# Graph attention by slots: order of the work within a slot, group of the weighting, length of the gather ring

## The chip, the cores and the metric

The kernel runs on one core of a Trainium2 chip. The metric is the device time in microseconds (us) of one execution. Engines are called by their names: TensorE (PE in the profile), VectorE (DVE), ScalarE (ACT), GpSimd (POOL) and SyncE (SP).

## What is computed

A stack of four graph layers over 3125 nodes of 256 features and 53125 edges: a weighted convolution with a small MLP, a second convolution that sums encoded edges, three blocks of typed attention (8 heads of 32) with an MLP each, and one last attention with edge features. Edges are sorted by their target. Cut to the step that matters, an attention over the edges that end in a node:

```python
score = (q[dst] * k[src]).sum(-1)                  # per edge and head
m     = segment_max(score, dst)
e     = exp(score - m[dst])
out   = segment_sum(e[:, :, None] * v[src], dst) / segment_sum(e, dst)
```

In the last layer the product is of a query with an edge's code, a term per source node is added, and a leaky ReLU stands before the maximum.

## The kernel before

Edges are packed into NT = 464 tiles of 128. Four tiles are a quad, four quads (WT = 16 tiles) a group; there are WG = 29 groups, so 116 quads. Each pair of tiles belongs to one block of 128 target nodes, whose number stands in a table (`c.block_i`) that engines read into registers at run time (`load_blocks`, L69). `attend` (L1399) is called four times: three typed calls, called L2a, and one with edge codes, called L3a. The instructions are written out in full; the code loops in Python only.

Per quad GpSimd gathers the rows of keys and values by four indirect DMAs (L1460) into a ring of `ring` buffers (10, or 11 in the last call), and waits for `weighted_ready` of the quad that held the buffer before. ScalarE widens two byte masks, `turned` (L1709) and `hot` (L1717). TensorE multiplies `turned` with the query block (`ask`, L1754), VectorE multiplies that with the gathered keys (`product`, L1513) and sums over a head (`reduce`, L1519). Per group a chain of maxima follows over 16 x 8 sequences of 128 edges: `flatten` (a transpose on TensorE, L1774), two scans (`scan_up` L1550, `scan_down` L1555), `spread_ends` (L1560), `sequence` on TensorE (L1779), two short scans along the group (`chain_up` L1566, `chain_down` L1572), `grow` (L1579), `expand` on TensorE (L1784), `pick_own` to `lower` (L1584 to L1604), and `unflatten` on TensorE (L1790, L1792). ScalarE takes the exponential (`soften`, L1729) and writes it into the extra columns of `weighted`. VectorE multiplies the gathered values with it (`weigh`, L1615), TensorE sums by target (`total`, L1765, two results per quad), VectorE adds each to the accumulator of its block (`add`, L1544) and, once per group, rescales one block (`rescale`, L1625).

Every engine has its order written out by hand. One pass of the loop is a slot. In slot n VectorE does the products and sums over heads of group n, the chain and the weightings of group m = n - 1, and additions of groups m - 1 and m. The chain's instructions stand one by one between additions and sums over heads; the four weightings follow in the second half of the slot, each followed by an addition, the rescale, or the next product. `weighted` holds one whole group, `prods` has two buffers and `score` one. TensorE's queries run two quads ahead of the product that reads them, and the totals of a quad follow its weighting.

## Time and profile before

| | |
|---|---|
| median of 3 runs | 5544.4 us (5542.47 to 5549.68) |
| profiled execution, span from first to last instruction | 6456.7 us |
| its own time beside the span | none given |
| instructions | 68859 |

The page gives, for the one profiled execution, the busy time of each engine and its share of the span, the busy share in 40 slices, the DMA queues, and groups of instructions with the mean duration of one, the idle time of the engine just before them and who ended most of it. The three runs of the table were taken apart from that execution.

### The profile page before, as it was taken

Reading aid. Unit: us, or ns where it says so; the run is one execution under the profiler, and the core shown is the slowest. Engines: PE = TensorE matmul, PEld = TensorE weight load, DVE = VectorE, ACT = ScalarE, POOL = GpSimd, SP = SyncE. Lnnn points to the kernel's source line nnn. Section 1 sums busy time; section 2 is a strip of 40 time slices with the busy share of each in tenths; the row PEclk is TensorE's granted clock in tenths of the full one; section 3 lists DMA queues with packets and bytes.
Section 4 is the critical chain, followed back from the end, with each engine's and each line's share of the span. In section 5 each row is a group of like instructions: output and inputs, shape, how many; then the busy total and the mean of one; then the engine's idle time right before and its main releaser. Section 6 shows DMA issues by size and latency. Waiting matters only on the chain. (4 is left out here: it accounts for less than half of the span.)

```text
span 6456.7 us, 68859 instructions
## 1 busy us (share of the span) xinstructions
PE 4457.4 (69%) x19341; PEld 3493.0 (54%) x19341; DVE 3832.0 (59%) x8692; ACT 1605.5 (25%) x3882; POOL 3364.1 (52%) x3108
## 2 busy tenths in 40 slices
PE   5666664577766666778857767796766679766776
PEld 4455453444436455557845555685555558545554
DVE  7544443544455666675347766643766776567777
ACT  3433332200004111113421211243211214312221
POOL 2588886366644555541356555134555530256663
PEclk9888887788888778779977777898778779878887
DMA  3688887255556555542266556315556541256664
GB/s 139 121 124 125 121 125 150 81 184 184 182 165 208 168 173 181 181 144 58 81 189 182 174 175 181 89 56 165 169 175 182 176 147 39 80 168 183 195 192 134
DMA packets 508435, 959.75 MB, mean 149 GB/s; under 512 B 85846, under 2 KB 298020, under 8 KB 507251
## 3 DMA queue, kind: packets, MB, share of 16 engines
q0 software_dynamic: 224512, 549.90, 34.1%
q1 hardware_dynamic: 283426, 404.92, 19.6%
q8 instruction: 170, 2.79, 0.2%
q14 instruction: 199, 1.62, 0.1%
q10 hardware_dynamic: 128, 0.52, 0.0%
HBM read 718.56 MB, written 236.50 MB: 148 GB/s over the span
## 5 line engine op out<-in xcount | busy, mean ns | idle before, releaser
L1460 POOL DMA_INDIRECT L2a_rows<-kv_rows,typed_index x960 | 966.3, 1007 | 627.8 <-DVE L2a_weighted L1615 349.9
L1765 PE MATMUL L2a_sums<-L2a_weighted,L2a_hot 128*128 128x264 f32 x2784 | 830.5, 450 | 166.8 <-DVE L2a_weighted L1615 159.4
L1754 PE MATMUL L2a_query<-x,L2a_turned 128*128 x2784 | 819.8, 447 | 55.8 <-ACT L2a_turned L1709 33.0
L867 POOL DMA_INDIRECT sum_rows<-L0s_rows,L0s_row_of x464 | 724.6, 1562 | 152.9 <-issue 119.4
L1765 PEld LDWEIGHTS L2a_sums<-L2a_weighted,L2a_hot 128*128 128x128 f32 x2784 | 591.2, 221 | 314.5 <-DVE L2a_weighted L1615 186.2
L1754 PEld LDWEIGHTS L2a_query<-x,L2a_turned 128*128 128x128 f32 x2784 | 627.2, 229 | 181.4 <-issue 62.5
L1460 POOL DMA_INDIRECT hold<-kv_rows,typed_index x432 | 445.4, 1031 | 449.8 <-DVE L2a_weighted L1615 279.5
L1460 POOL DMA_INDIRECT L3a_rows<-feature_rows,index x464 | 489.1, 1054 | 301.7 <-DVE L3a_weighted L1615 155.1
L1285 POOL DMA_INDIRECT L1s_rows<-rows,index x464 | 451.0, 972 | 351.2 <-issue 133.8
L1717 ACT ACTIVATE L2a_hot<-L2a_hot 128x512 f32<-128x512 uint8 x348 | 218.7, 629 | 1470.8 <-PE L2a_sums L1765 726.6
L1002 PE MATMUL L0s_message<-features,L0s_share 128*128 x928 | 312.8, 496 | 285.9 <-ACT L0s_share L967 285.9
L2296 POOL TENSOR_SCALAR L2d_here<-hold,mask 128x256 f32<-128x256 f32 x200 | 183.1, 933 | 552.6 <-DVE hold L2372 404.5
L1342 PE MATMUL L1s_code_ps<-L1s_wide,L1s_fields 128*128 128x512 f32 x464 | 285.8, 702 | 219.3 <-DVE L1s_code L1311 138.4
L1519 DVE TENSOR_REDUCE L2a_score<-L2a_prods 128x32 f32<-128x1024 f32 x348 | 417.8, 1201 | 0.4
L1002 PEld LDWEIGHTS L0s_message<-features,L0s_share 128*128 128x128 f32 x928 | 215.3, 242 | 364.9 <-issue 329.1
L1765 PE MATMUL L3a_sums<-L3a_weighted,L3a_hot 128*128 128x264 f32 x928 | 282.7, 457 | 92.6 <-DVE L3a_weighted L1615 89.3
L1709 ACT ACTIVATE L2a_turned<-L2a_turn 128x512 f32<-128x512 uint8 x348 | 216.9, 624 | 507.7 <-PE L2a_query L1754 191.8
L1513 DVE TENSOR_TENSOR L2a_prods<-L2a_query,L2a_rows 128x1024 f32<-128x1024 f32 x240 | 291.9, 1216 | 76.5 <-remote 47.3
L901 DVE TENSOR_TENSOR L0s_hot<-count,early 128x512 f32<-128x512 f32 x116 | 80.5, 694 | 419.0 <-ACT L0s_hot L980 412.7
L1305 DVE TENSOR_TENSOR acc<-acc,L1s_sums 128x256 f32 x232 | 97.4, 420 | 378.4 <-remote 176.5
L1544 DVE TENSOR_TENSOR acc<-acc,L2a_sums 128x264 f32 x696 | 290.4, 417 | 10.8 <-PE L2a_sums L1765 9.1
L1615 DVE TENSOR_TENSOR L2a_weighted<-L2a_rows,L2a_weighted 128x1024 f32<-128x1024 f32 x240 | 292.4, 1218 | 3.4 <-ACT L2a_weighted L1729 1.3
(428 smaller groups left out, 8550.9 us busy)
## 6 DMA issues: line engine op xcount, KB each, us to landing
code_rows<-L1s_code SPq DMA_DIRECT2D x116, 512.0 KB
L3a_code<-code_rows SPq DMA_DIRECT2D x116, 512.0 KB
L0s_wide<-source_rows SPq DMA_DIRECT2D x116, 256.0 KB
L2a_turn<-turned_rows SPq DMA_DIRECT2D x87, 256.0 KB
L2a_pens<-mask_rows SPq DMA_DIRECT2D x87, 256.0 KB
L2a_hot<-hot_rows SPq DMA_DIRECT2D x87, 256.0 KB
kv_rows<-L2d_key_rows SPq DMA_DIRECT2D x50, 384.0 KB, 2.6
kv_rows<-L2d_value_rows SPq DMA_DIRECT2D x150, 128.0 KB, 2.4
```

The costliest lines, as they stand in the source:

```text
L867: pool.indirect_dma_start(c.sum_rows[u], bass.IndirectOffsetOnAxis(ap=row_of[:, 4 * n + u:4 * n + u + 1], axis=0), rows[n % ring][:, u, :] ...
L1002: last = pe.matmul(message[n % 2][:, u, :], share[n % 2][:, u, :], at(c.q, b[i])[:, 0:D], start=True, stop=True)
L1285: pool.indirect_dma_start(rows[n % ring][:, u, :], None, table, bass.IndirectOffsetOnAxis(ap=c.index[:, t:t + 1], axis=0)).then_inc(landed ...
L1342: pe.matmul(code_ps[j % 2][:, :, :].rearrange("p k d -> p (k d)"), fields[g % 2][:, :], wide[:, 2 * j % FT:2 * j % FT + 2, :].rearrange("p ...
L1460: pool.indirect_dma_start(rows[n % ring][:, u, :], None, table, bass.IndirectOffsetOnAxis(ap=index_of[:, t:t + 1], axis=0)).then_inc(lande ...
L1513: dve.tensor_tensor(prods[q % 2][:, :, :], query[q % 2][:, :, :], other, ALU.mult).then_inc(multiplied, 1)
L1519: last = dve.tensor_reduce(own.rearrange("p k h -> p (k h)"), prods[q % 2][:, :, :].rearrange("p k (h d) -> p (k h) d", h=H), AX.X, ALU.add)
L1544: dve.tensor_tensor(at(c.acc, b), at(c.acc, b), sums[(m * WP + j) % held][:, :], ALU.add).then_inc(added, 1)
L1615: dve.tensor_tensor(weighted[:, 4 * q:4 * q + 4, :].rearrange("p k (h d) -> p k h d", h=H)[:, :, :, 0:HD], rows[quad % ring][:, :, values: ...
L1717: act.activation(hot[quad % 2][:, :, :].rearrange("p u e -> p (u e)"), hot8[m % 2][:, q * 4 * P:(q + 1) * 4 * P], ACT.Copy).then_inc(hot_r ...
L1754: last = pe.matmul(query[q % 2][:, u, :], turned[quad % 2][:, u, :], at(c.q, b[2 * q + u // 2]), start=True, stop=True)
L1765: last = pe.matmul(sums[(m * WP + j) % held][:, :], hot[quad % 2][:, j % 2 * 2 + k, :], weighted[:, 2 * j + k, :], start=k == 0, stop=k == 1)
```

## The change

The loops over groups become loops over quads, and each slot of VectorE becomes four stretches that all begin in the same way. A product is followed directly by its sum over heads, from a single `prods` buffer; two additions stand together; the chain of the previous group is cut into three: both long scans and the ends behind the first quad, the short scans and the gap behind the second, the rest behind the third. The weighting works two groups (8 quads, `late`) behind the product, where it was one group behind, and comes before the product of its stretch (after it in the fourth). `weighted` becomes three buffers of one quad (`kept`), and the exponentials get tiles of their own (`prob`, two), from which ScalarE copies the extra columns (`column`). The shrink factors are copied from PSUM by ScalarE (`keep_shrink`) before VectorE's `rescale` reads them. `score` gets two buffers. The ring becomes 12 buffers (13 in the last call). TensorE's queries stay two quads ahead, between the two totals of a quad. SyncE's loads of edge codes are spread over the slot. The loop runs WG + 3 times on VectorE. In `load_blocks` VectorE reads 8 values per slot, where it read 16. `reduce` of the last call holds the small addition that was `join`. The core of the diff:

```diff
-    held, codes = 3, 4
+    held, codes, late, kept, quads = 3, 4, 2 * WQ, 3, WG * WQ
     with Stage(nc, name) as st:
-        ring = RQ if typed else 11
+        ring = 12 if typed else 13
...
-        weighted = st.sb("weighted", [P, WT, VC])
-        prods = [st.sb(f"prods{k}", [P, 4, D]) for k in range(2)]
-        score = st.sb("score", [P, WT, H])
+        weighted = [st.sb(f"weighted{k}", [P, 4, VC]) for k in range(kept)]
+        prods = st.sb("prods", [P, 4, D])
+        score = [st.sb(f"score{k}", [P, WT, H]) for k in range(2)]
+        prob = [st.sb(f"prob{k}", [P, WT, H]) for k in range(2)]
...
+            def product(g):
+                if g < quads:
+                    wait(dve, query_ready, g + 1)
+                    wait(dve, score_ready if typed else summed, g)
+                    if typed:
+                        wait(dve, landed[g % ring], 64 * (g // ring + 1))
+                        other = rows[g % ring][:, :, 0:D]
+                    else:
+                        wait(dve, code_landed[g % codes], 16 * (g // codes + 1))
+                        other = code[g % codes][:, :, :]
+                    dve.tensor_tensor(prods[:, :, :], query[g % 2][:, :, :], other, ALU.mult).then_inc(multiplied, 1)
+            def reduce(g):
+                if g < quads:
+                    n, q = g // WQ, g % WQ
+                    wait(dve, multiplied, g + 1)
+                    own = score[n % 2][:, 4 * q:4 * q + 4, :]
+                    last = dve.tensor_reduce(own.rearrange("p k h -> p (k h)"),
+                                             prods[:, :, :].rearrange("p k (h d) -> p (k h) d", h=H), AX.X, ALU.add)
+                    if typed:
                         last.then_inc(score_ready, 1)
...
+            def add(w, k, b):
+                if 0 <= w < quads:
+                    j = 2 * w + k
+                    wait(dve, sums_ready, j + 1)
+                    wait(dve, added, j)
+                    if w % WQ == 0 and k == 0:
+                        wait(dve, rescaled, w // WQ)
+                    dve.tensor_tensor(at(c.acc, b), at(c.acc, b), sums[j % held][:, :], ALU.add).then_inc(added, 1)
...
+            def weigh(w):
+                if 0 <= w < quads:
+                    q = w % WQ
+                    wait(dve, prob_ready, w // WQ + 1)
+                    wait(dve, sums_ready, 2 * (w - kept + 1))
+                    dve.tensor_tensor(
+                        weighted[w % kept][:, :, :].rearrange("p k (h d) -> p k h d", h=H)[:, :, :, 0:HD],
+                        rows[w % ring][:, :, values:values + D].rearrange("p k (h d) -> p k h d", h=H),
+                        prob[w // WQ % 2][:, 4 * q:4 * q + 4, :].unsqueeze(3).broadcast_to([P, 4, H, HD]), ALU.mult
+                    ).then_inc(weighted_ready, 1)
...
+            for n in range(WG + 3):
+                m, g = n - 1, n * WQ
+                chain, tail = 0 <= m < WG, n >= 2
+
+                if tail:
+                    blocks = load_blocks(nc, mybir.EngineType.DVE, c, (n - 2) * WP - 2, WP)
+                else:
+                    blocks = [0] * WP
+                weigh(g - late)
+                product(g)
+                reduce(g)
+                add(g - late - 1, 0, blocks[0])
+                add(g - late - 1, 1, blocks[1])
                 if chain:
                     scan_up(m)
                     scan_down(m)
                     spread_ends(m)
+                weigh(g + 1 - late)
+                product(g + 1)
+                reduce(g + 1)
+                rescale(n - 2, blocks[2])
+                add(g - late, 0, blocks[2])
+                add(g - late, 1, blocks[3])
                 if chain:
                     chain_up(m)
                     chain_down(m)
                     grow(m)
+                weigh(g + 2 - late)
+                product(g + 2)
+                reduce(g + 2)
+                add(g + 1 - late, 0, blocks[4])
+                add(g + 1 - late, 1, blocks[5])
                 if chain:
                     pick_own(m)
                     join_own(m)
                     reach_first(m)
                     reach_last(m)
                     spread_fall(m)
                     lower(m)
+                product(g + 3)
+                reduce(g + 3)
+                weigh(g + 3 - late)
+                add(g + 2 - late, 0, blocks[6])
+                add(g + 2 - late, 1, blocks[7])
...
+            def keep_shrink(m):
+                if 0 < m < WG:
+                    wait(act, shrink_ready, m)
+                    wait(act, rescaled, m - 1)
+                    act.activation(shrink[:, :], shrink_ps, ACT.Copy).then_inc(shrink_kept, 1)
+
+            def column(w):
+                if 0 <= w < quads:
+                    q = w % WQ
+                    wait(act, prob_ready, w // WQ + 1)
+                    wait(act, sums_ready, 2 * (w - kept + 1))
+                    act.activation(weighted[w % kept][:, :, HD::HC], prob[w // WQ % 2][:, 4 * q:4 * q + 4, :], ACT.Copy
+                                   ).then_inc(column_ready, 1)
...
+                total(g - late, 0)
+                ask(g + 2, near[0], near[1])
+                total(g - late, 1)
+                sequence(m)
+                total(g + 1 - late, 0)
+                ask(g + 3, near[2], near[3])
+                total(g + 1 - late, 1)
+                expand(m)
+                total(g + 2 - late, 0)
+                ask(g + 4, near[4], near[5])
+                total(g + 2 - late, 1)
+                unflatten(m)
+                ask(g + 5, near[6], near[7])
+                flatten(n)
+                total(g + 3 - late, 0)
+                total(g + 3 - late, 1)
```

## Rows read from the trace of the kernel before

**Rows 1.** The page of the kernel before: span, and busy time by engine.
```profile
span 6456.7 us, 68859 instructions
PE 4457.4 (69%) x19341; PEld 3493.0 (54%) x19341; DVE 3832.0 (59%) x8692; ACT 1605.5 (25%) x3882; POOL 3364.1 (52%) x3108
```

**Rows 2.** Busy time by stretch, middle of first and last attention call.
```profile
core 0: us, PE busy (x) PEld busy (x) DVE busy (x) ACT busy (x) POOL busy (x), PEclk, DMA share, GB/s
2200.00:2880.00 680.00, 479.17 (x1748) 370.89 (x1747) 471.72 (x802) 132.28 (x243) 392.25 (x385) 0.79 0.59 177
...
5750.00:6400.00 650.00, 455.96 (x1767) 356.97 (x1766) 489.21 (x928) 135.56 (x244) 407.53 (x383) 0.82 0.63 188
```

**Rows 3.** Timeline: a small TensorE matmul and the VectorE scan waiting for it.
```profile
2512.62 0.22 PE L1779 MATMUL L2a_small<-L2a_ends,head 128*8 128x32 f32 x2
...
2520.60 0.27 DVE L1566 TENSOR_TENSOR_SCAN L2a_up<-links,L2a_up,L2a_small 8x32 f32<-8x32 f32 x1 [6.79 <-remote]
```

**Rows 4.** Timeline of GpSimd, sixteen gathers of one slot and the next first.
```profile
2499.98 0.94 POOL L1460 DMA_INDIRECT hold<-kv_rows,typed_index  x1 [7.21 <-DVE L2a_weighted L1615]
2501.23 1.90 POOL L1460 DMA_INDIRECT hold<-kv_rows,typed_index  x1 [0.30 <-issue]
...
2519.91 0.94 POOL L1460 DMA_INDIRECT L2a_rows<-kv_rows,typed_index  x1 [0.30 <-issue]
2528.45 0.94 POOL L1460 DMA_INDIRECT L2a_rows<-kv_rows,typed_index  x1 [7.59 <-DVE L2a_weighted L1615]
```

**Rows 5.** Waits of GpSimd: first call, last call, then everything before attention.
```profile
POOL L2a_rows L1460 <- DVE L2a_weighted L1615: 116.6, 16, 7.8
...
POOL hold L1460 <- DVE L2a_weighted L1615: 92.0, 11, 18.5
...
POOL L3a_rows L1460 <- DVE L3a_weighted L1615: 155.1, 27, 22.0
...
POOL L1s_rows L1285 <- remote: 62.1, 25, 6.7
POOL L1s_rows L1285 <- PE L1s_sums L1353: 27.6, 22, 2.7
POOL sum_rows L867 <- ACT L0s_rows L961: 21.9, 34, 11.9
POOL sum_rows L867 <- DMA sum_rows<-L0s_rows,L0s_row_of: 11.6, 38, 0.3
```

**Rows 6.** Timeline of VectorE: neighbours that don't depend on each other.
```profile
2533.64 1.22 DVE L1519 TENSOR_REDUCE L2a_score<-L2a_prods 128x32 f32<-128x1024 f32 x1
2534.77 1.22 DVE L1615 TENSOR_TENSOR L2a_weighted<-L2a_rows,L2a_weighted 128x1024 f32<-128x1024 f32 x1
2535.90 0.42 DVE L1544 TENSOR_TENSOR acc<-acc,L2a_sums 128x264 f32 x1
2536.24 1.22 DVE L1513 TENSOR_TENSOR L2a_prods<-L2a_query,L2a_rows 128x1024 f32<-128x1024 f32 x1
```

**Rows 7.** Timeline of VectorE: dependent neighbours, at fill, first chain, and the end.
```profile
2073.59 1.23 DVE L1513 TENSOR_TENSOR L2a_prods<-L2a_query,hold 128x1024 f32<-128x1024 f32 x1 [2.67 <-DMA hold<-kv_rows,typed_index]
2074.84 1.22 DVE L1519 TENSOR_REDUCE L2a_score<-L2a_prods 128x32 f32<-128x1024 f32 x1
...
2121.16 0.42 DVE L1550 TENSOR_TENSOR_SCAN L2a_climb<-L2a_pens,L2a_small 128x128 f32<-128x128 f32 x1 [14.21 <-remote]
2121.61 0.42 DVE L1555 TENSOR_TENSOR_SCAN L2a_most<-L2a_pens,L2a_climb 128x128 f32<-128x128 f32 x1
...
2124.29 0.20 DVE L1566 TENSOR_TENSOR_SCAN L2a_up<-links,L2a_small 8x32 f32<-8x32 f32 x1
2124.53 0.21 DVE L1572 TENSOR_TENSOR_SCAN L2a_tops<-links,L2a_up 8x32 f32<-8x32 f32 x1
...
2907.65 0.43 DVE L1544 TENSOR_TENSOR acc<-acc,L2a_sums 128x264 f32 x1 [0.21 <-DVE acc L1544]
2908.29 0.43 DVE L1544 TENSOR_TENSOR acc<-acc,L2a_sums 128x264 f32 x1 [0.21 <-DVE acc L1544]
```

More of the change, by code:

```diff
@@ L1425, in attend @@
         gap, fall, diag = st.sb("gap", [H, 1]), st.sb("fall", [H, 1]), st.sb("diag", [H, H])
+        shrink = st.sb("shrink", [P, H])
         pick, other = st.sb("pick", [P, 2, WT]), st.sb("other", [P, 2])
@@ new lines, in load_code @@
+            def load_code(g):
+                if not typed and g < quads:
+                    wait(sp, multiplied, g - codes + 1)
+                    sp.dma_start(code[g % codes][:, :, :], c.code_rows[:, 4 * g:4 * g + 4, :]
+                                 ).then_inc(code_landed[g % codes], 16)
+            load_turn(0)
+            for g in range(codes - 1):
+                load_code(g)
+            load_turn(1)
+            for n in range(WG + 1):
+                load_code(n * WQ + 3)
+                load_pens(n)
+                load_code(n * WQ + 4)
+                load_hot(n - 1)
+                load_code(n * WQ + 5)
+                load_turn(n + 2)
+                load_code(n * WQ + 6)
@@ L1674, in _ @@
                     lower(m)
-                if more:
-                    product(n, 2)
-                if tail:
-                    add(m - 1, 7, before[7])
-                if chain:
-                    weigh(m, 0)
-                    rescale(m, now[0])
-                if more:
-                    reduce(n, 2)
-                if chain:
-                    weigh(m, 1)
-                    add(m, 0, now[0])
-                if more:
-                    product(n, 3)
-                    join(n, 2)
@@ new lines, in column @@
+            def column(w):
+                if 0 <= w < quads:
+                    q = w % WQ
[3 more added lines that the diff above has]
+                                   ).then_inc(column_ready, 1)
+            for g in range(3):
+                turn(g)
+            for n in range(WG + 2):
+                m, g = n - 1, n * WQ
+                for s in range(WQ):
+                    widen(g + s - late + 1)
+                    turn(g + s + 3)
+                    if s == 2:
+                        drop(m)
+                    if s == 3:
+                        soften(m)
+                        keep_shrink(m)
+                    column(g + s - late + 1)
@@ new lines, in total @@
+            def total(w, k):
+                if 0 <= w < quads:
+                    j = 2 * w + k
+                    wait(pe, weighted_ready, w + 1)
+                    wait(pe, column_ready, w + 1)
+                    wait(pe, hot_ready, w + 1)
+                    wait(pe, added, j - held + 1)
+                    for u in range(2):
+                        last = pe.matmul(sums[j % held][:, :], hot[w % 2][:, 2 * k + u, :],
+                                         weighted[w % kept][:, 2 * k + u, :], start=u == 0, stop=u == 1)
@@ L1827, in _ @@
-            for j in range(6, WP):
-                total(WG - 1, j)
+                if 0 <= m < WG:
+                    wait(pe, zz_ready, m + 1)
+                    if m:
+                        wait(pe, diag_ready, m)
+                        pe.matmul(shrink_ps, first_hot[m % 2][:, :], diag[:, :], start=True, stop=True
+                                  ).then_inc(shrink_ready, 1)
+                    pe.transpose(below_ps, zz[:, :], c.ident[:, :]).then_inc(below_ready, 1)
+            near = load_blocks(nc, mybir.EngineType.PE, c, 0, WQ)
```

297 lines of the change are left out of this document (79 added, 218 removed).

## The prediction

> **What bounds the kernel now.** I read the page's totals first, then the busy times by stretch, the waits of GpSimd, the timeline of one slot on GpSimd, VectorE and TensorE, and last the starts of neighbouring VectorE instructions, which give prices.
>
> The page shows a span of 6456.7 us with VectorE at 59% and GpSimd at 52% [rows 1]. The median of the three runs shown is 5544.4 us. The page gives no other time for the profiled execution than its span, so 912.3 us lie between the profiled execution and a plain one, and before anything is priced one has to know where they sit. In 680 us in the middle of the first attention call GpSimd issued 385 gathers, which is 24.1 slots of 16, so a slot took 28.2 us; VectorE was busy 471.7 us of it, 19.6 us per slot [rows 2]. In the last call (feature rows) 383 gathers in 650 us give 27.2 us per slot, VectorE 20.4 us.
>
> What is VectorE doing in the other 8 us? In the slot at 2512 us the little matmul of line 1779 stands at 2512.62 us for 0.22 us, and the scan that waits for nothing but it starts at 2520.60 us, after 6.79 us idle with no releaser that this trace can name ("remote") [rows 3]. The same kind of gap sits before the scan or before the pick of line 1584 in almost every slot. TensorE's update comes late, although its record does not.
>
> GpSimd shows what this costs. One slot of gathers runs from 2499.98 us, mostly 0.95 us each with 0.30 us between two of them (one of them 1.90 us), to 2520.85 us, and then GpSimd waits 7.59 us for a weighting to free a buffer [rows 4]. So a slot of gathers takes 20.0 us (16 x 1.25) to 21.2 us (20.87 plus 0.30); I take 20.8. Those waits sum to 116.6 + 92.0 = 208.6 us in the first call and 155.1 us in the last; the second and third calls are built like the first, so 3 x 208.6 + 155.1 = 781 us. The gathers and scatters of the two layers before them add 62.1 + 27.6 + 21.9 + 11.6 = 123 us of waiting on the same engine [rows 5]. The sum, 904 us, is almost exactly the missing 912 us. I read this as follows: the late TensorE updates belong mainly to the profiled execution, and in a plain one the attention calls run at GpSimd's rate, 20.8 us per slot (21.3 us in the last call, where a gather means 407.5 / 383 = 1.06 us against 392.3 / 385 = 1.02 us [rows 2]), with VectorE's 19.6 us plus its own short waits just below it. That is the base from which I price the change.
>
> The Trainium skill (NOTIFIC — the notification-queue block, section 7.1 Overflow) says that the internal pipeline that writes trace records never drops one and may hold up the engine instead. That fits the gap, with its 6.79 us beside it, but no row shows the cause, and no term below uses it.
>
> **The change, part by part.** Everything that the change removes from VectorE is waiting; the arithmetic stays: four products, four sums over heads, four weightings, eight additions, one rescale and one chain of maxima per slot. What changes is who stands next to whom, and that has a price in this trace.
>
> Independent neighbours overlap. A sum over heads starts at 2533.64 us, a weighting at 2534.77, an addition at 2535.90, a product at 2536.24: 1.13, 1.13 and 0.34 us from start to start, each about 0.08 us before its forerunner's record ends [rows 6]. Dependent neighbours do not. A product followed at once by its own sum takes 1.25 us to the next start, so 0.12 us more. Two additions in a row whose sums are there take 0.64 us (2907.65 to 2908.29), so 0.30 us more: the second waits for the first's count and only then works out its block's address. The two scans in a row take 0.45 us (2121.16 to 2121.61), about 0.12 us more than their overlapping neighbours by the same pattern, and the two short scans 0.24 us (2124.29 to 2124.53), about 0.1 us more [rows 7].
>
> - **Products next to their sums, one product buffer.** 4 x 0.12 = 0.48 us per slot. The wait for the previous sum costs nothing, because a weighting of 1.13 us lies between (three quads of four) or 2 us of chain.
> - **Additions in pairs.** Four pairs, 4 x 0.30 = 1.20 us. The rescale now stands directly ahead of the first addition of its group, which waits for it: another 0.30 us (bounds 0.1 and 0.3).
> - **The chain in thirds.** Scan on scan and ends on scan, 2 x 0.12 = 0.24 us; the short scans and the gap about 0.15 us.
> - **Register loads of the block table.** 8 values instead of 16 on VectorE. The load used to be mostly hidden; now it stands behind an addition that itself waits, so I expect it in the open, 0 to 0.7 us, taken as 0.2 us, as no row of the groups shows it alone.
> - **ScalarE** gets four column copies and one copy of the shrink factors per slot. It is busy 132 us in 680, 5.5 us per slot [rows 2]; even 5 x 0.4 us leaves it under 8 us. Behind its new waits stand the widenings and turnings, each two quads early. I cost it at nothing; what hides it is VectorE's 22 us.
> - **TensorE** does the same matmuls and queries now run two quads ahead of the product that reads them. By the order written out, every result is asked for at least 4 us after its matmul is issued. Cost nothing; if that cover went, its busy 479 us in 680, 19.9 us per slot at the granted mean of 0.79 [rows 2], would be next.
> - **Longer ring and SyncE's order.** GpSimd gets 12 or 13 buffers, of which 8 quads are held by the later weighting: four to five quads, 20 us, of lead. Its own work stays at 20.8 us. The loads keep a group's lead. Nothing.
>
> Sum for VectorE in a typed call: 19.6 + 0.48 + 1.50 + 0.39 + 0.2 = 22.2 us; adding the same starts instruction by instruction through the new slot gives 21.9. I take 22.0 us. In the last call the small addition after each sum becomes its direct neighbour too, 4 x 0.12, so from 20.4 us it goes to 23.1 us (the sum is 20.4 + 2.6 + 0.5 = 23.5, I shade it by the same 0.3).
>
> Against the gatherer's 20.8 and 21.3 us the slot becomes longer by 1.2 and 1.8 us. The first two slots of a call run at GpSimd's rate in either kernel, so 27 slots count: 3 x 27 x 1.2 + 27 x 1.8 = 97 + 49 = 146 us. The end of a call gets longer as well: after the last product the old kernel has one chain, four weightings and their additions, some 19 us; the new one has eight weightings and sixteen additions, about 12.5 + 10 + 2 = 24.5 us. That is 5.5 x 4 = 22 us. Together 168 us. Taking the trace's own time as the base of the gatherer's rate instead (28.2 less the 7.6 us wait, 20.6 us per slot) moves this by 20 us either way. 5544.4 + 168 is 5712; I write 5710 us.
>
> **Weighing a rule.** The Trainium skill (VectorE: DVE Perf Modes, section The DRAIN you can't avoid) says that a next VectorE instruction starts only when the pipe is empty and that a semaphore between two adds nothing. Rows 6 and 7 disagree: 1.13 us without the dependence, 1.25 us with it. By the rule all the neighbour terms would be nil and the result would be that of the first rival.
>
> **The rivals.**
> *GpSimd keeps the bound.* If dependent neighbours cost nothing in the new order, VectorE needs 19.6 us, stays under 20.8 us, and only the longer end counts: 5544 + 22 = 5566 us, or 5545 if the end hides as well. Against it: the 0.64 us between additions repeats. Chance 0.13. The skill's DRAIN rule, named above, would lead here.
> *The late updates are real.* If TensorE's updates come late in plain runs too, say by half of the 7.6 us, a slot now takes 24.5 us; the new order asks for each result 4 to 10 us later than it is issued and would swallow that, so a slot falls to 22.2 us: 27 x 4 x 2.3 = 248 us gained, less 22, about 5320 us. It decides from the point where the present plain slot exceeds 22 us. For it: rows 3 show a wait that really held VectorE. Against it: GpSimd's waits already fill the 912 us, and no other place in the trace could give back that much. At a quarter instead of a half the two kernels tie. Chance 0.22, and about 0.05 more for a tie.
> *TensorE becomes the bound.* At the lower of its clock's two levels (1.2 and 2.4 GHz) its matmuls would need over 30 us per slot; if the new gaps lower the granted mean from 0.79 to 0.7, it needs 22.5 us plus waits: 5800 us and more. Chance 0.08.
> That the change doesn't do what it says (weighting not late) can be excluded by the diff.
>
> **How the numbers follow.** The forecast has 0.52 and a range of its own from 5630 us (no load shown, rescale at 0.1 us, slots of 21.4 us) to 5800 us (load at 0.7 us, gathers at 20.0 us so that VectorE's about 20.4 us was the old bound). The range for 8 in 10 takes in the first rival and about half of the faster one: 5430 to 5810 us. A measurement of this kernel can tell about 0.2% from no change, 11 us. Slower by more: forecast, TensorE case and most of the first rival, 0.72; within: 0.06; faster: 0.22.
>
> **What would show it.** In the profile after: VectorE's additions 0.64 us apart in pairs and product to sum 1.25 us; VectorE busy share up, its waits before the scan and the pick gone or much smaller; slots of the profiled execution shorter than 28.2 and 27.2 us, because the slack swallows the late updates, although the plain time rises; GpSimd still waiting for weightings. It is wrong if plain time falls: then the plain runs had waits that I ascribe to the profiled execution alone.

## The result and the profile after

| | before | after |
|---|---|---|
| median, same chip | 5547.0 us (4 runs, 5542.5 to 5551.9) | 5863.7 us (4 runs, 5860.6 to 5864.9) |
| ratio | 1 | 1.0567, 95% interval 1.0552 to 1.0582 |
| span of the profiled execution | 6456.7 us | 5861.4 us |

The change makes the kernel 5.7% slower, by 317 us, where 166 us (5710 less 5544.4) were forecast. The profiled execution of the kernel after is no special one: its own time is 5863.05 us. That of before was (6456.7 us against 5544.4 us), and run e1 below takes its place. The page's totals of the kernel after, where [rows 1] stood for before:

```profile
span 5861.4 us, 71363 instructions
PE 4302.7 (73%) x19341; PEld 3231.5 (55%) x19341; DVE 3960.7 (68%) x8692; ACT 1645.1 (28%) x4458; POOL 3428.9 (58%) x3108
```

Busy time by stretch, in the middle of the first and of the last attention call (the columns are those of [rows 2]):

```profile
2200.00:2600.00 400.00, 309.38 (x1239) 217.33 (x1237) 349.01 (x565) 98.44 (x255) 295.08 (x275) 0.98 0.75 215
5300.00:5600.00 300.00, 225.28 (x853) 155.33 (x854) 258.68 (x448) 68.72 (x180) 199.58 (x190) 0.95 0.66 200
```

From the start of the third product of one slot to that of the next, the mean over the 27 steady slots of a call is 23.3 us in the three typed calls and 25.2 us in the last. VectorE is busy 87% of the first stretch; TensorE's granted clock is 0.98 there, near the upper level (2.4 GHz). Who waits for whom in the first call (us in total, times, longest):

```profile
DVE L2a_weighted L1625 <- PE L2a_sums L1761: 34.2, 22, 1.6
DVE acc L1552 <- DVE acc L1552: 19.8, 92, 0.6
...
POOL L2a_rows L1462 <- DVE L2a_weighted L1625: 26.9, 18, 1.6
```

GpSimd waits for VectorE, and VectorE waits for two things only: 0.21 us between the additions of a pair, as priced, and 1.6 us once per slot before a weighting. The profile puts the latter down to TensorE's results. The timeline of VectorE at that place shows what it is:

```profile
2502.19 1.22 DVE L1530 TENSOR_REDUCE L2a_score<-L2a_prods 128x32 f32<-128x1024 f32 x1
2503.33 1.21 DVE L1625 TENSOR_TENSOR L2a_weighted<-L2a_rows,L2a_prob 128x1024 f32<-128x1024 f32 x1
2504.46 0.42 DVE L1552 TENSOR_TENSOR acc<-acc,L2a_sums 128x264 f32 x1
2505.09 0.43 DVE L1552 TENSOR_TENSOR acc<-acc,L2a_sums 128x264 f32 x1 [0.21 <-DVE acc L1552]
2507.08 1.23 DVE L1625 TENSOR_TENSOR L2a_weighted<-hold,L2a_prob 128x1024 f32<-128x1024 f32 x1 [1.55 <-PE L2a_sums L1761]
```

The additions stand 0.63 us apart. From the second one to the weighting it is 1.99 us, and between them the program has nothing but `load_blocks`. The trace keeps a record of the register load itself, which the profile doesn't count as busy: 1.84 us for 8 values. TensorE's results were there before: the second addition had already waited for a later one than the weighting needs. The view of line 71, `load_blocks`, has these loads, as minimum, median and maximum in ns. In the kernel before, where they are of 16 values, and in the kernel after:

```profile
L71 DVEq TENSOR_LOAD <-block_i x29: 597/1100/1118, 2088.8 to 2891.7; - x29
...
L71 DVEq TENSOR_LOAD <-block_i x28: 1840/1846/1853, 2061.6 to 2669.9; - x28
```

In the last call the sum over heads, its small addition (L1538) and the leaky ReLU (L1543) wait for one another:

```profile
5402.49 1.22 DVE L1530 TENSOR_REDUCE L3a_score<-L3a_prods 128x32 f32<-128x1024 f32 x1
5403.81 0.19 DVE L1538 TENSOR_TENSOR L3a_score<-L3a_score,L3a_rows 128x32 f32<-128x32 f32 x1
5404.04 0.29 DVE L1543 SCALAR_TENSOR_TENSOR L3a_score<-L3a_score 128x128 f32<-128x128 f32 x1
```

That is 1.32 us from the sum to its addition and 0.23 us from there on, 0.3 us per quad more than 1.13 us [rows 6] and some 0.1 us (an estimate) for independent neighbours.

### The profile page after: what moved, and what is told of

Same layout as the page of the kernel before. It is cut to its first block and busy times, and to the rows that moved or that the text cites. A ratio compares the mean times of both kernels' runs of the same rounds, so it can differ in the third digit from the quotient of the medians.

```text
span 5861.4 us, 71363 instructions
## 1 busy us (share of the span) xinstructions
PE 4302.7 (73%) x19341; PEld 3231.5 (55%) x19341; DVE 3960.7 (68%) x8692; ACT 1645.1 (28%) x4458; POOL 3428.9 (58%) x3108
## 5 line engine op out<-in xcount | busy, mean ns | idle before, releaser
L1462 POOL DMA_INDIRECT L2a_rows<-kv_rows,typed_index x1032 | 1103.1, 1069 | 385.1 <-issue 297.1
L1761 PE MATMUL L2a_sums<-L2a_weighted,L2a_hot 128*128 128x264 f32 x2784 | 773.0, 407 | 292.0 <-DVE L2a_weighted L1625 273.5
L1749 PE MATMUL L2a_query<-x,L2a_turned 128*128 x2784 | 753.8, 418 | 162.1 <-DVE L2a_prods L1523 97.5
L1761 PEld LDWEIGHTS L2a_sums<-L2a_weighted,L2a_hot 128*128 128x128 f32 x2784 | 505.0, 194 | 475.3 <-DVE L2a_weighted L1625 366.1
L1749 PEld LDWEIGHTS L2a_query<-x,L2a_turned 128*128 128x128 f32 x2784 | 540.9, 204 | 349.3 <-issue 278.3
L1462 POOL DMA_INDIRECT hold<-kv_rows,typed_index x360 | 375.8, 1044 | 152.7 <-issue 152.7
L1625 DVE TENSOR_TENSOR L2a_weighted<-L2a_rows,L2a_prob 128x1024 f32<-128x1024 f32 x258 | 313.8, 1216 | 89.7 <-PE L2a_sums L1761 89.4
L1353 PE MATMUL L1s_sums<-L1s_rows,L1s_hot 128*128 128x256 f32 x928 | 255.0, 399 | 136.9 <-issue 107.9
L1761 PE MATMUL L3a_sums<-L3a_weighted,L3a_hot 128*128 128x264 f32 x928 | 267.8, 419 | 115.4 <-DVE L3a_weighted L1625 101.8
L1353 PEld LDWEIGHTS L1s_sums<-L1s_rows,L1s_hot 128*128 128x128 f32 x928 | 174.2, 196 | 297.5 <-issue 224.1
L1749 PE MATMUL L3a_query<-hold,L3a_turned 128*128 x928 | 257.7, 426 | 46.3 <-DVE L3a_prods L1523 24.8
```

Source lines behind the costliest of these rows:

```text
L1353: last = pe.matmul(sums[j % held][:, 0:D], hot[n % hots_held][:, u, :], rows[n % ring][:, u, :], start=k == 0, stop=k == 1)
L1462: pool.indirect_dma_start(rows[g % ring][:, u, :], None, table, bass.IndirectOffsetOnAxis(ap=index_of[:, t:t + 1], axis=0)).then_inc(lande ...
L1625: dve.tensor_tensor(weighted[w % kept][:, :, :].rearrange("p k (h d) -> p k h d", h=H)[:, :, :, 0:HD], rows[w % ring][:, :, values:values ...
L1749: last = pe.matmul(query[g % 2][:, u, :], turned[g % 2][:, u, :], at(c.q, second if u // 2 else first), start=True, stop=True)
L1761: last = pe.matmul(sums[j % held][:, :], hot[w % 2][:, 2 * k + u, :], weighted[w % kept][:, 2 * k + u, :], start=u == 0, stop=u == 1)
```

## The experiments

Each time is compared with the kernel before on the same chip and in the same batch of runs. Runs e1 to e8 share one chip, e9 to e11 a second, e12 to e15 a third, e16 and e17 a fourth.

**e1: the kernel before, profiled again.** No edit.

> The kernel before, unchanged, for a second profile. The record's theory (the late TensorE updates belong to that one profiled execution, a plain one runs at GpSimd's rate): a span near 5545 us, slots of 20.8 us in the typed calls and 21.3 us in the last, and hardly any wait of GpSimd for a weighting. First rival (the late updates come with every profiled execution of this order): a span near 6450 us again. Second rival (VectorE, not GpSimd, holds the plain slot): a span near 5545 us with GpSimd still waiting 1 us or more in each slot.

It took 5558.9 us (5548.3 us the median of seven others) with a span of 5557.2 us: profiling costs at most 0.2%. Totals by stretch, then the waits of VectorE and of GpSimd in the first call:

```profile
2200.00:2600.00 400.00, 332.86 (x1367) 256.41 (x1366) 367.94 (x636) 106.72 (x189) 296.62 (x296) 0.93 0.77 231
5300.00:5600.00 300.00, 191.42 (x763) 146.51 (x761) 228.84 (x424) 57.31 (x103) 163.44 (x157) 0.90 0.56 170
...
DVE L2a_prods L1513 <- DMA L2a_rows<-kv_rows,typed_index: 22.5, 21, 2.8
DVE L2a_prods L1513 <- DMA hold<-kv_rows,typed_index: 7.6, 7, 2.1
...
POOL L2a_rows L1460 <- issue: 85.0, 279, 0.3
POOL hold L1460 <- issue: 36.6, 120, 0.3
```

GpSimd never waits for anybody, VectorE waits for the gathered rows, and no update of TensorE comes more than 0.9 us after its instruction. For the profile of [rows 3] the updates can't tell this: that trace has 45827 records of semaphore changes and this one 84800, and some of VectorE's and ScalarE's are missing too. The starts can. There the scan behind `sequence` begins in the median 2.9 us, and up to 8.0 us, after both its matmul and VectorE's instruction before it have ended, and the pick behind `expand` 4.2 us, and up to 8.6 us; in e1 neither is ever over 0.1 us late. The slot is 20.9 us in the typed calls and 21.5 us in the last. So GpSimd sets the pace, at the rates that the prediction took as its base, but the 912 us don't come from profiling.

**e2: the register load aligned.** The places of the table are counted from its start, where four spare ones (`GP`) stand ahead of the first block. The kernel after loads eight values that begin 2 past a multiple of 8; e2 loads ten from the multiple of 8 itself, of which the last eight are used.

```diff
-                    blocks = load_blocks(nc, mybir.EngineType.DVE, c, (n - 2) * WP - 2, WP)
+                    blocks = load_blocks(nc, mybir.EngineType.DVE, c, (n - 2) * WP - GP, WP + 2)[2:]
```

> The changed kernel, where VectorE's register load starts two values earlier, on a multiple of eight, and takes ten values instead of eight. Theory (the load of 1.84 us is long because of where it starts, and 1.55 us of it are idle time of VectorE in each of 116 slots): the load takes 0.6 to 1.1 us as the other loads do, the idle time falls to 0.4 to 0.8 us, the kernel to 5735 to 5775 us. Rival (the length goes with VectorE's state, or the wait is for TensorE's totals as the profile names it): the load stays at 1.8 us or the idle time stays, 5850 to 5870 us.

5784.4 us, ratio 1.0420 (1.0402 to 1.0437). That is 9 us above the range expected. The load takes 1.07 us instead of 1.84 us for two more values, and the slot falls by 0.7 to 0.8 us, to 22.6 us (24.4 us in the last call): here each microsecond of the load is a microsecond of the slot. In the attention calls of these traces VectorE's loads take 0.6 us for 8 values and 1.10 us for 16, both from 4 past a multiple of 8, 1.07 us for 10 from a multiple of 8, and 1.84 us for 8 from 2 past one. So every short one starts on a multiple of 4. Start and length aren't all of it: in the layer before attention the loads of 8 values from 4 past a multiple of 8 take anything from 0.59 to 1.65 us, and no run shows why.

**e3: the load hidden.** The same load, issued after the fourth sum of the slot before, where VectorE has work queued that doesn't need it.

```diff
-                if tail:
-                    blocks = load_blocks(nc, mybir.EngineType.DVE, c, (n - 2) * WP - 2, WP)
-                else:
-                    blocks = [0] * WP
+                blocks = following
...
+                if 1 <= n < WG + 2:
+                    following = load_blocks(nc, mybir.EngineType.DVE, c, (n - 1) * WP - GP, WP + 2)[2:]
                 weigh(g + 3 - late)
```

> The changed kernel with the same aligned load issued before the fourth weighting of the slot before, where a weighting of 1.13 us and a sum cover it. Theory (exposed load is the term that was mis-sized, 1.63 us per slot): all of it goes, 116 x 1.63 = 189 us, to about 5675 us; VectorE's slot 21.7 us and 23.6 us in the last call. Rival (something else stands behind it at once, such as TensorE's totals): 5735 us or more.

5812.3 us, ratio 1.0470 (1.0452 to 1.0487), 0.5% slower than e2, where 5675 us were expected: a miss. VectorE's own work is less, but the slot is 22.9 us. GpSimd is the one that holds it (16 x (1.13 + 0.30) = 22.9 us), because its gathers grew. Its timeline next to VectorE's weightings, then its totals of 500 us (busy, mean ns | idle before), which in e1 are 1003 ns:

```profile
2511.46 1.22 DVE L1625 TENSOR_TENSOR L2a_weighted<-hold,L2a_prob 128x1024 f32<-128x1024 f32 x1
2511.68 1.82 POOL L1462 DMA_INDIRECT L2a_rows<-kv_rows,typed_index  x1 [0.30 <-issue]
2513.80 0.94 POOL L1462 DMA_INDIRECT L2a_rows<-kv_rows,typed_index  x1 [0.30 <-issue]
...
L1462 POOL DMA_INDIRECT L2a_rows<-kv_rows,typed_index x264 | 298.0, 1129 | 80.5 <-issue 80.5
L1462 POOL DMA_INDIRECT hold<-kv_rows,typed_index x86 | 97.5, 1134 | 26.2 <-issue 26.2
```

A gather that starts 0.2 us after a weighting takes 1.82 us, that is until 0.8 us after the weighting has ended; the next takes 0.94 us. Over the 500 us gathers that overlap a weighting mean 1.42 us, the others 0.97 us. Wherever within a weighting a gather starts, it ends 0.82 us after the weighting (102 gathers of e3's first call, nine in ten of them within 0.01 us of it). Which of them meet depends on how the two engines' rhythms fall on each other, and so the order of VectorE sets the price of a gather.

**e4: dependent neighbours apart**, the load in its old place and length. One addition moves between each product and its sum, the rescale ahead of its product.

```diff
+                add(g - late - 1, 0, blocks[0])
                 reduce(g)
-                add(g - late - 1, 0, blocks[0])
                 add(g - late - 1, 1, blocks[1])
...
```

> The changed kernel with the first addition of each pair between the product and its sum over heads, and the rescale ahead of the product; late weighting, ring, chain in thirds and the misaligned load stay. Theory (a dependent neighbour costs 0.12 us at a product and 0.29 us at an addition): 4 x 0.12 + 4 x 0.29 + 0.2 = 1.8 us per slot, and as the last addition no longer holds the instruction queue, about 1 us of the load is covered too, so the slot would be 20.4 us and meets GpSimd's 20.8 us: 5560 to 5600 us. Rival (the rule that a semaphore between two VectorE instructions adds nothing): at most 20 us gained, 5845 us.

5618.7 us, ratio 1.0127 (1.0110 to 1.0144). Over three quarters of the loss are gone, with not one instruction fewer. That is not the neighbours alone: VectorE goes from the last addition of a slot to the weighting of the next in 0.34 us, where the kernel after took 1.99 us, although the load between them still takes 1.84 us.

```profile
2271.89 0.41 DVE L1552 TENSOR_TENSOR acc<-acc,L2a_sums 128x264 f32 x1
2272.23 1.21 DVE L1625 TENSOR_TENSOR L2a_weighted<-hold,L2a_prob 128x1024 f32<-128x1024 f32 x1
```

The record of this load runs from 2269.94 to 2271.78 us, while VectorE is at the sum and the weighting ahead of these two. So this order hides the whole load, where about 1 us of it was expected. The time is 19 us above the upper expectation, because the slot (21.3 us) is GpSimd's now, with gathers of 1.02 us.

**e5: the kernel before with half of the sums' work left out.** The sums over heads read 16 of 32 products.

```diff
-                                         prods[q % 2][:, :, :].rearrange("p k (h d) -> p (k h) d", h=H), AX.X, ALU.add)
+                                         prods[q % 2][:, :, :].rearrange("p k (h d) -> p (k h) d", h=H)[:, :, 0:HD // 2],
+                                         AX.X, ALU.add)
```

> The kernel before, where the sum over a head (line 1519) adds 16 of its 32 products: part of the computation left out, so that VectorE has about 0.55 us less to do four times per slot, 2.2 us of its 19.3 us. Theory (GpSimd's gathers hold the slot at 21 us, VectorE only waits longer for rows): no more than 0.5% off, 5520 to 5560 us. Rival (VectorE's own chain holds it): 116 x 1.4 to 2.2 us less, 5290 to 5385 us.

5693.9 us, ratio 1.0248 (1.0216 to 1.0280): less work for VectorE makes the kernel slower, which neither side had expected. Its waits and GpSimd's totals:

```profile
DVE L2a_prods L1513 <- DMA L2a_rows<-kv_rows,typed_index: 71.0, 44, 4.8
...
L1460 POOL DMA_INDIRECT L2a_rows<-kv_rows,typed_index x250 | 274.2, 1097 | 76.2 <-issue 76.2
```

VectorE waits for rows three times as long as in e1 (94.8 against 30.1 us, both row buffers together), and the gathers mean 1.09 us instead of 1.00 us: those that meet a weighting meet it earlier in its course and are held up longer.

**e6 and e7: the weights of the weighting out of SBUF.** e7 lets ScalarE write them to PSUM, so that the weighting has one SBUF input; that leaves room for two result buffers only, and e6 is the kernel before with two (`held`), its control.

```diff
-    held, codes = 3, 4
+    held, codes = 2, 4
...
-                    weighted[:, 4 * q:4 * q + 4, HD::HC].unsqueeze(3).broadcast_to([P, 4, H, HD]), ALU.mult
+                    prob_ps[:, 4 * q:4 * q + 4, :].unsqueeze(3).broadcast_to([P, 4, H, HD]), ALU.mult
```

> The kernel before with two PSUM buffers for the totals instead of three: the control for the next run, which needs the third bank. Both theories: the same or up to 3% slower, 5545 to 5710 us; the gathers' lengths unchanged (mean 1.00 us).

> The control, and ScalarE writes the exponentials a second time, into the freed PSUM bank, from which VectorE's weighting reads them: one SBUF input instead of two, the same arithmetic. Theory (a gather that meets a weighting is held up by it, since both want the same way into SBUF, 1.4 us against 0.97 us without in the run with the hidden load): the gathers all take 0.95 us, GpSimd's slot falls from 21.0 to 20.1 us, and the kernel is 40 to 100 us faster than the control. Rival (long gathers come from full DMA queues): lengths as in the control, and the kernel 10 to 40 us slower than it, for the second exponential of 0.4 us in the chain.

e6 took 5669.2, 5669.7 and 5705.7 us (ratio 1.0233, 1.0190 to 1.0275); a fourth one took 12633 us, is left out and stays unexplained. e7 took 5661.0 us (1.0182, 1.0159 to 1.0204). In e7 the gathers take 947 ns in the mean, against 1010 ns in e6, and 2 of 372 take over 1 us. So a weighting with both inputs in SBUF is what stretches them. The time hardly moves: the intervals of the two ratios overlap, and 40 to 100 us were expected. With two result buffers VectorE waits for the maxima in both ("DVE L2a_pick <- PE L2a_small" 51.9 us in 24 times in e6, 43.5 us in 25 times in e7, absent in e1), and in e7 GpSimd waits for weightings: this order with two buffers can't use the faster gathers.

The Trainium skill (SBUF — State Buffer, section SBUF: two separate sides) describes such a lock: VectorE and GpSimd share a pair of ports, and of an instruction of VectorE with two SBUF inputs and one of GpSimd that reads SBUF, whichever starts first has the pair for its whole length, while the other waits. The rows agree for the gather, which reads its row numbers from a table in SBUF: one that starts within a weighting waits for its end. By the page the gather shown above would lose the time to the end of the weighting, 1.0 us (an estimate); it loses 0.87 us (1.82 less 0.95). For the other half the rows don't agree: 47 weightings of e3's first call start while a gather runs, and they start no later and take no longer (1.21 us) than the others.

**e8: e4 and e3 together.**

> The changed kernel with neighbours apart and the load aligned and hidden, both edits together. VectorE needs about 19.7 us a slot by the two earlier runs. Theory (from there on GpSimd holds the slot, and its gathers are stretched by weightings): no better than with the neighbours apart alone, 5570 to 5640 us, VectorE waiting 1 to 2 us per slot for rows. Rival (VectorE still holds it): 116 x 0.4 us less than with the neighbours apart alone, 5570 us, and with a GpSimd that keeps 20.8 us per slot, 5545 us.

5656.0 us, ratio 1.0169 (1.0149 to 1.0190), slots of 21.4 us, gathers of 1.03 us: 16 us above the range expected and 0.4% above e4. The load was hidden in e4 already, and the floor is GpSimd's, so there was nothing left for this edit to gain.

**e9 to e11: the mended order**, on a chip where the kernel before takes 6488.2 us (6470 to 6497). e9 is e8 with the join of the last call apart from its sum and the fourth weighting ahead of the fourth product; e10 adds the weights in PSUM to it, with two result buffers; e11 is e5 with the weights in PSUM and two result buffers.

> The changed kernel with four edits to VectorE's order: neighbours apart, load aligned and hidden, the fourth weighting ahead of its product, and the small addition of the last call behind an addition of totals instead of directly behind its sum over heads (there 1.30 us from start to start). Weightings still read two SBUF tiles. Theory (GpSimd with stretched gathers holds the typed calls; only the last call gets better, by up to 1.2 us in 29 slots): 5600 to 5650 us. Rival (VectorE's order is all that matters): below the kernel before, 5500 to 5540 us.

> The same, and the weighting reads the exponentials from a PSUM bank of their own, which the totals give up (two buffers instead of three); ScalarE copies them there once per group. The same arithmetic. Theory (a weighting with two SBUF inputs stretches gathers; with one it doesn't, and the later weighting gives TensorE's results room enough for two buffers): gathers of 0.95 us, 20.0 us of GpSimd per slot, VectorE 19.6 to 20.8 us: a slot of 20.2 us, 21 us in the last call, 5440 to 5490 us, faster than the kernel before. Rival (two buffers for the totals make VectorE wait as they did in the old order): 5560 us or more, with waits for totals of 1 us and more per slot.

> The kernel before with sums over 16 of 32 products (part of the computation left out), two buffers for the totals, and the exponentials read from PSUM. With the short sums alone the kernel took 5694 us and its gathers 1.09 us in the mean. Theory (that slowdown is gathers held up by weightings, which came closer together): gathers of 0.95 us, GpSimd's slot 20.0 us, kernel 5440 to 5500 us. Rival (the short sums cost time in some other way, such as colder TensorE or full DMA queues): 5640 us or more.

6252.8 us (ratio 0.9634, 0.9618 to 0.9650), 6361.3 us (0.9802, 0.9786 to 0.9819) and 7202.3 us (1.1096, 1.1077 to 1.1114). Readers of TensorE's results start late in these traces too; waits of VectorE in e9:

```profile
DVE acc L1557 <- remote: 70.0, 23, 5.0
DVE acc L1557 <- PE L2a_sums L1770: 39.0, 29, 4.5
```

158 of its 928 additions of totals start over 1 us, and up to 6.7 us, after both their matmul and VectorE's instruction before have ended; in e1, e8 and the kernel after no update of TensorE comes over 0.9 us late. The 6488 us are unprofiled runs, so such times come in any execution on such a chip. That the 6457 us of the profile of before come from one too is likely, not shown: the record doesn't name its chip. An order with more lead between a matmul and its reader is better there (e9), with one result buffer fewer less so (e10), and the old order with short sums, weights in PSUM and two result buffers is far worse (e11).

**e12 to e15: the same again**, on a chip where the kernel before takes 5544.9 us; e12 is the kernel after.

> The changed kernel, unaltered. If the chip has no late TensorE updates (kernel before at 5545 to 5560): 5864, ratio 1.057 as in the result. If it has them (kernel before at 6450 to 6500): theory A, that the kernel before pays for them because its sums wait for a product and its weighting for a result of TensorE only just done, while the changed order has two groups of slack, expects a ratio below 1, 6200 to 6400 us, ratio 0.96 to 0.99. Theory B, that late updates cost both orders alike, expects about 6800, ratio 1.05.

> The changed kernel with its register load aligned and issued a step earlier, its dependent neighbours of VectorE apart, and its join of the last call apart from its sum (the edit of e9). Chip without late updates: theory A, VectorE's own work sets the slot, expects VectorE at 19.6 busy and 20.3 per slot, 5480 to 5540. Theory B, the gathers stretched by the weightings set a floor of 21.3 to 21.5 per slot as in e4 and e8, expects 5600 to 5650, ratio 1.010 to 1.018. Chip with late updates: as e9, ratio 0.963.

> The same, with the weights of the weighting read from PSUM, where ScalarE copies them (the edit of e10). Chip without late updates: theory B expects that gathers of 0.95 us give the floor back, 20.2 to 20.8 per slot, 5440 to 5560, ratio 0.98 to 1.0; theory A, which gives the weightings no part in it, expects no difference from e13 within 0.3%. Chip with late updates: as e10, ratio 0.980.

> The kernel before with the sums of 16 of its 32 products per slot left out, and the weights of the weighting read from PSUM (the edit of e11). Chip without late updates: if stretched gathers were all that made e5 slower than before, the slot is GpSimd's own 20.2 us and the time 5400 to 5500, ratio 0.975 to 0.99. If a chain through TensorE and ScalarE that the product's buffers close is the floor besides, as e7's waits of the pick for the maxima suggest, 5600 to 5680, ratio 1.01 to 1.025, with VectorE waiting for the maxima or for rows and GpSimd waiting for weightings. Chip with late updates: as e11, ratio 1.11.

| | us | ratio, 95% interval | slot typed, last | gathers |
|---|---|---|---|---|
| e12 after | 5871.0 | 1.0586 (1.0569 to 1.0604) | 23.3, 25.2 | 1.07 us |
| e13 mended order | 5635.9 | 1.0153 (1.0119 to 1.0186) | 21.6, 22.4 | 1.06 us |
| e14 with weights in PSUM | 5472.8 | 0.9865 (0.9849 to 0.9882) | 20.1, 20.5 | 0.95 us |
| e15 before, half sums, PSUM | 5511.4 | 0.9939 (0.9922 to 0.9956) | 20.6, 20.9 | 0.95 us |

e13 shows the floor of the stretched gathers, as its theory B had it, and e14 lifts it: 163 us between them for the place of one operand, in spite of one result buffer fewer and one more copy on ScalarE. GpSimd's rows of e14, totals and then waits:

```profile
L1465 POOL DMA_INDIRECT L2a_rows<-kv_rows,typed_index x304 | 288.3, 948 | 92.6 <-issue 90.8 <-DVE L2a_weighted L1633 1.8
...
POOL L2a_rows L1465 <- DVE L2a_weighted L1633: 1.8, 6, 0.3
```

16 x (0.95 + 0.30) = 20.0 us is its slot, and VectorE is busy 385.2 of 400 us in it: both are full. This version is faster than both kernels. e15 undoes the loss of e5 (from 1.0248 to 0.9939), though it too has one result buffer fewer. Against e7, from which it differs in the short sums alone, they gain 2.4% (1.0182 to 0.9939); with stretched gathers the same edit lost 2.5% (e5). It is 11 us slower than expected, and its VectorE waits for the maxima (56.0 us in 26 times), as in e6 and e7.

**e16 and e17: the weights in PSUM for the kernel after, and for e3.** Two result buffers again.

> The changed kernel with nothing altered but the place from which the weighting reads its weights: a copy in PSUM, made by ScalarE. Theory A, the changed kernel is held by VectorE's own instructions and its exposed register load, 23.3 us per slot, and the stretched gathers lie in GpSimd's spare time: gathers of 0.95 us, GpSimd waits longer for weightings (about 3 us per slot), time unchanged within 0.5%, 5840 to 5890, ratio 1.053 to 1.062. Theory B, that the gathers' stretching is part of the slowdown, expects 5650 to 5750, ratio 1.02 to 1.037.

> The changed kernel with its register load issued a step earlier (the edit of e3) and the weights read from PSUM. Theory A, in e3 the slot was held by gathers that the weightings stretched: gathers of 0.95 us, VectorE at 20.4 us busy with its short gaps gives 21.0 to 21.5 us per slot, 22.5 to 23 in the last call, 5640 to 5700, ratio 1.017 to 1.028. Theory B, e3 was held by something else (a cycle of buffers through TensorE and ScalarE), expects e3's 22.9 us per slot again and 5790 to 5830, ratio 1.044 to 1.051.

e16: 5909.4 us, ratio 1.0642 (1.0615 to 1.0668). The gathers are at 0.95 us and the kernel after gains nothing; it is 19 us above the upper expectation and loses another 0.5 us per slot, since with two result buffers the additions wait for TensorE ("DVE acc <- PE L2a_sums" 17.3 us in 22 times, absent in the kernel after). So the stretched gathers are no part of the slowdown as it stands. e17: 5741.8 us, ratio 1.0354 (1.0327 to 1.0380), neither theory's number. The slot is 21.9 us, against 22.9 us in e3, and GpSimd waits for VectorE again, 2 us per slot. The place of the load, on VectorE's timeline:

```profile
2504.62 0.43 DVE L1555 TENSOR_TENSOR acc<-acc,L2a_sums 128x264 f32 x1 [0.21 <-DVE acc L1555]
2504.97 1.21 DVE L1628 TENSOR_TENSOR L2a_weighted<-L2a_rows,L2a_own_bank 128x1024 f32<-128x1024 f32 x1
```

0.35 us instead of 1.99 us. So the gathers did hold e3, as theory A had it. The expected time was too low because VectorE's slot without its load is 21.9 us, not 21.0 to 21.5 us, and in the last call, where the joins hold VectorE, 24.5 us, not 22.5 to 23 us.

## Why the prediction was right in direction and wrong in size

- **Base of 20.8 and 21.3 us per slot, GpSimd's rate**: right, 20.9 and 21.5 us in e1.
- **"The late TensorE updates belong mainly to the profiled execution"**: wrong. GpSimd's waits did fill the 912 us, so they sat where the prediction put them, but that doesn't say why. e1 has none although it is profiled, and unprofiled runs on another chip are as slow. What was taken for one kernel in two modes was most likely one kernel on two chips (the chip of the first profile isn't on record). The number for the base survived, since the median came from an undisturbed chip. The note on trace records that was set beside it explains nothing here.
- **Neighbours: 0.48 us for products, 1.20 for additions, 0.30 for the rescale, 0.39 for the chain**: right. Product to sum is 1.25 us, addition to addition 0.63 us, scan to scan 0.45 us; rescale to addition is 0.56 us, 0.22 more than the 0.34 of independent ones. With the load taken out and the gathers freed (e17) the typed slot is 21.9 us, and the 22.0 us of the prediction less its 0.2 us for the load are 21.8. In the typed calls e14 differs from e17 only in VectorE's order, with the neighbours of products, sums and additions apart and the fourth weighting ahead of its product, and its slot is 20.1 us, GpSimd's floor: at least 1.8 us are theirs. The 245 us that come back in e4 are neighbours and load together.
- **Register load, 0.2 us, bounds 0 to 0.7**: this is the term that was mis-sized. That it would stand in the open was foreseen; its length was wrong. It costs 1.55 us per slot, twice its upper bound. What was missed is the start: 16 values of the kernel before took 1.10 us, but these 8 start 2 past a multiple of 8 in the table and take 1.84 us. 22.0 - 0.2 + 1.55 = 23.35 us; measured 23.3. The groups of the page have no row of the load, but the view of line 71 has one. For the layer before attention of the kernel before, where the loads are of 8 values, it shows 28 of them from 0.59 to 1.65 us, and that would have been a wider bound. In the attention calls of the kernel before the load is hidden (VectorE's idle time behind it is 0 in the median), so no idle time there could show its price.
- **Last call, 0.12 us per quad for the join**: 0.3 us, two waits in a row instead of one. 23.1 + 1.35 + 0.72 = 25.2 us; measured 25.2.
- **End of a call, 5.5 us more**: from the last product to the last addition it is 23.9 us before and 31.8 us after, 7.9 us more (7.6 in the last call), partly the same load.
- **GpSimd's "own work stays at 20.8 us"**: wrong as a rule, harmless here. Its gathers mean 1.08 us instead of 1.00 in the kernel after, 22.1 us per slot, still under VectorE's 23.3.
- **TensorE, ScalarE, ring, SyncE at nothing**: right; neither VectorE nor GpSimd waits for them (the wait laid to TensorE is the load), and TensorE's granted clock rose from 0.93 to 0.98 in the first call.
- **The sum**: 97 + 49 + 22 = 168 us predicted. Measured (23.29 - 20.94) x 81 = 190, (25.21 - 21.53) x 27 = 99, ends 32: 321 us by these parts, 316 us by the four calls from first product to last addition, 317 us in the medians.
- **Rivals.** GpSimd doesn't keep the bound, and by the Trainium skill's DRAIN rule (VectorE: DVE Perf Modes, The DRAIN you can't avoid) a semaphore between two adds nothing and the neighbour terms would be nil, which the starts above and e14 against e17 contradict. The same section says that a next instruction that isn't held starts earlier, and with that the 1.13 us of independent neighbours agree. The late updates are real in plain runs, but on another chip; there the mended order gains 3.7%, as that rival argued. Whether the change itself gains there wasn't tried. TensorE didn't become the bound.

So the step that failed is the register load's 0.2 us, with bounds of 0 and 0.7 us that came from no row: the 1.35 us that it lacked, times 108 slots, are 146 us, and the range left 100 us above the forecast.

## What to carry to other kernels

A wait or a gap that is moved into the open has to be priced by its own length, also where the profile doesn't count it: register loads first of all, with their start and length. The order of the neighbours decides whether it is in the open: the same load of 1.84 us costs 1.55 us behind an addition that waits for its neighbour, and nothing in e4. When the bound is shared by two engines, an instruction of one can lengthen those of the other, so less work on one may cost time (e5): look at the mean duration of the same instruction in both traces. And a profiled span far from the median calls for a second profile before any of it is used as the base.

## What the runs showed of the hardware

- In the attention calls a register load on VectorE takes 0.6 us for 8 values and 1.10 us for 16 from 4 past a multiple of 8 in the table, 1.07 us for 10 from a multiple of 8, and 1.84 us for 8 from 2 past one. In the layer before, loads of 8 took 0.59 to 1.65 us from the same kind of start, cause open. The waits give the gap to the wrong releaser.
- An indirect gather issued on GpSimd takes 0.95 us alone. If it starts within a weighting with both inputs in SBUF it ends 0.82 us after the weighting, so that it takes up to 2.0 us. A weighting that starts within a gather is not held up. With one input in PSUM the gathers mean 0.95 us.
- On one chip of four VectorE started up to 6.7 us (e9) after a matmul that it needed and its own instruction before had ended (6488 us instead of 5545 to 5557 us for the kernel before, the chip's cause unknown), and kernels rank differently there: e10 is behind e9 by 1.7%, where on another chip e14, the same kernel as e10, is ahead of e13, the same as e9, by 2.9%.
